# Cross-attention with keys turned before they are stored, a fifth chunk of probabilities turned by DMA, and normalisation once a head

## The reference

```python
q = (x @ Wq + bq); k, v = split(cond @ Wkv + bkv)          # x is layer-normed
q = q / sqrt(64)
q = fq_sym(q, axis=-1); k = fq_sym(k, axis=-1); v = fq_sym(v, axis=2)   # round(x / s) * s, s = max|x| / 127
attn = softmax(q @ k.T); attn = fq_unsigned(attn)          # s = max / 255
x = x + (attn @ v) @ Wp + bp
x = x + causal_self_attention_with_rope(layernorm(x))      # 128 tokens each
x = x + rmsnorm(swiglu_fp4(layernorm(x)))
```

## Time and profile before

| what | value |
|---|---|
| median of 3 executions (range) | 2946.23 us (2945.79 to 2947.63) |
| profiled execution: its time / its span | 2948.09 us / 2946.2 us |
| busy over the span: PE / DVE / ACT / POOL | 2612.4 / 1860.9 / 1033.5 / 553.9 us |
| keys and values end (last DVE instruction ends) | 1412.5 us from the span's start |
| cross-attention, first to last copy of scores | 1458.6 to 2154.8 us |
| last output of the cross-attention | 2175.5 us |

### The profile page before, as it was taken

How to read it: one execution, slowest core, us unless ns; L and a number is a source line. 1 busy time by engine, 2 the same in 40 slices (tenths; PEclk the granted TensorE clock), 3 DMA queues, 4 the chain that set the end, 5 groups by cost and what they waited for, 6 DMA issues and landing times. The chain is left out here.

```text
span 2946.2 us, 42369 instructions
## 1 busy us (share of the span) xinstructions
PE 2612.4 (89%) x16808; PEld 1327.1 (45%) x16808; DVE 1860.9 (63%) x2883; ACT 1033.5 (35%) x920; POOL 553.9 (19%) x208
## 2 busy tenths in 40 slices
PE   6999999999999999999377777777759999499998
PEld 3444444444444444444144444444444476244443
DVE  5855555555555555554489999999944343566663
ACT  3111111111111111111189999999962133211100
POOL 0500000000000000000256546645610721011100
PEclk9999999999999999999689999999989977699999
DMA  6121222212221222212479999999871300300000
GB/s 236 65 79 57 78 85 78 72 67 81 85 78 57 78 85 78 72 67 68 122 172 180 194 208 185 194 199 197 176 224 60 112 1 1 61 15 15 8 0 29
DMA packets 493040, 288.93 MB, mean 98 GB/s; under 512 B 403200, under 2 KB 468992, under 8 KB 488064
## 3 DMA queue, kind: packets, MB, share of 16 engines
q1 hardware_dynamic: 492928, 287.28, 37.5%
HBM read 117.37 MB, written 69.21 MB: 63 GB/s over the span
## 5 line engine op out<-in xcount | busy, mean ns | idle before, releaser
L456 PE MATMUL kv_acc<-kv_whi,kv_xthi 128*128 128x512 f16 x2048 | 776.8, 379 | 5.6 <-DVE kv_xtlo L500 5.6
L456 PE MATMUL kv_acc<-kv_wlo,kv_xthi 128*128 128x512 f16 x2048 | 776.7, 379 | 0.0
L456 PE MATMUL kv_acc<-kv_whi,kv_xtlo 128*128 128x512 f16 x2048 | 776.7, 379 | 0.0
L919 DVE TENSOR_SCALAR_CACHE_REDUCE at_sc<-at_score 128x1024 f32<-128x1024 f32 x512 | 612.0, 1220 | 47.8 <-PE at_score L812 43.4
L1005 ACT ACTIVATE at_sc<-at_sc,at_bias,at_qs 128x4096 uint16<-128x4096 f32 x128 | 484.8, 3791 | 13.4 <-DVE at_bias L931 13.4
L812 PE MATMUL at_score<-at_kt,at_q 128*128 128x512 f16 x1024 | 309.2, 392 | 88.0 <-DVE at_sc L919 43.1
L487 ACT ACTIVATE kv_parts<-kv_key 128x1024 f16<-128x1024 f32 x64 | 67.6, 1057 | 866.6 <-DVE kv_key L525 866.6
L456 PEld LDWEIGHTS kv_acc<-kv_whi,kv_xthi 128*128 128x128 f16 x2048 | 200.5, 98 | 247.9 <-DVE kv_xtlo L500 6.1
L456 PEld LDWEIGHTS kv_acc<-kv_whi,kv_xtlo 128*128 128x128 f16 x2048 | 200.5, 98 | 242.0 <-issue 0.8
L456 PEld LDWEIGHTS kv_acc<-kv_wlo,kv_xthi 128*128 128x128 f16 x2048 | 200.5, 98 | 241.8 <-issue 0.6
L506 DVE SCALAR_TENSOR_TENSOR kv_key<-kv_acc,kv_bias 128x512 f32<-128x512 f32 x128 | 88.5, 692 | 335.1 <-PE kv_acc L456 335.1
(11 more groups left out here) (181 smaller groups left out, 3285.0 us busy)
## 6 DMA issues: line engine op xcount, KB each, us to landing
kv_rows<-in_ctx SPq DMA_DIRECT2D x64, 512.0 KB, 6.0
key_rows<-kv_parts SPq DMA_DIRECT2D x64, 512.0 KB, 2.6
values<-kv_val SPq DMA_DIRECT2D x32, 1024.0 KB, 6.3
x<-values SPq DMA_DIRECT2D x16, 2048.0 KB, 8.8
wq_stage<-in_wkv SPq DMA_DIRECT2D x4, 2048.0 KB, 7.8
x<-in_x SPq DMA_DIRECT2D x2, 2048.0 KB, 8.2
wq_stage<-in_wq SPq DMA_DIRECT2D x2, 2048.0 KB, 13.1
wt_stage<-in_wp SPq DMA_DIRECT2D x2, 2048.0 KB, 10.1
```

Of the source, the lines that this page charges most:

```text
L456: last = nc.tensor.matmul(acc[c][:], a[s][:, k, :], b[:, c, k, :], start=(k == 0 and q == 0), stop=(k == KD - 1 and q == 2))
L919: nc.vector.tensor_scalar(sc[n % 2][:, c * SC:(c + 1) * SC], score[pos % 2][:], 1.0, None, ALU.mult, ALU.max, accum_out=part_max[n % 2][:, ...
```

## The change

- Each key tile is turned by a DMA transpose in SBUF during the projection (`turn_keys`), both tiles of a pair are stored turned (runs of 512 bytes), and the attention loads key quarters with plain DMAs. Head 0's keys are loaded during the projection, those of the last two tiles straight from SBUF (`own_keys`).
- The queries' 64 transposes move into the last pair of the projection, with ACT evicting them.
- The block value_scales is gone. Its reduction stands at the start of the attention; the scales reach all partitions by 16 PE transposes of a broadcast column and two ACT evictions, not through DRAM. DVE, after its first ten copies, and ACT, before its first exponential, wait for the projection's last stores.
- Of each unit a fifth chunk (the last 1024 columns of the second half, the "tail") is turned by a DMA of its own, issued as the last thing of the unit in SP's order. PE turns three chunks instead of four. ACT evicts two or three of them, DVE the middle one in slots with even `n` alone.
- Sum, inverse and output are made once a head (four units), and POOL multiplies by the value scales as it moves the output out.
- The values get a buffer of their own, and head 0's keys take the room of `x`. Before the end `x` is loaded again, as it was before.

```diff
--- before.py
+++ after.py
-            def store_keys(u, s):
+            def turn_keys(u, s):
                 sp.wait_ge(parts_ready, u + 1)
-                dst = kt_d[bass.ds(u, 1)].rearrange("a p n -> (a p) n")
-                sp.dma_start(dst, parts[s][:].rearrange("p h c d -> p (h c d)")).then_inc(k_stored[s], 16)
+                sp.sem_inc(keys_begun, 1)
+                sp.dma_start_transpose(kt[:, :, s * P:(s + 1) * P], parts[s][:].rearrange("p h c d -> p (h c d)"))\
+                    .then_inc(keys_turned[s], 16)
+
+            def store_keys(i):
+                for s in range(2):
+                    sp.wait_ge(keys_turned[s], 16 * (i + 1))
+                    sp.sem_inc(keys_begun, 1)
+                dst = kt_d[:, :, bass.ds(i * (2 * P), 2 * P)].rearrange("h p n -> p h n")
+                sp.dma_start(dst, kt[:]).then_inc(k_stored, 16)
 
             def body(i, first, last):
                 if not last:
                     for s in range(2):
                         sp.wait_ge(lo_ready, 2 * i + s + 1)
                         load(ctx_d[bass.ds(2 * i + 2 + s, 1)].rearrange("a p k n -> (a p) k n"), s)
+                if not first:
+                    sp.wait_ge(k_stored, 16 * i)
+                    sp.sem_inc(keys_begun, 1)
                 for s in range(2):
-                    store_keys(2 * i + s, s)
-                sp.wait_ge(v_ready, 2 * i + 2)
+                    turn_keys(2 * i + s, s)
+                    if last:
+                        heads.own_keys(sp, 2 * i + s, parts[s][:, 0].rearrange("p c d -> p (c d)"))
+                if not last:
+                    store_keys(i)
+                sp.wait_ge(taken, NC * (2 * i + 2))
                 dst = v_d[:, :, bass.ds(2 * i, 2), :].rearrange("h p a d -> p h a d")
                 sp.dma_start(dst, val[:]).then_inc(v_stored, 16)
-
-            each_pair(sp, body)
...
+            quarter = KVT // 8
+            body(0, True, False)
+            for n in range(4):
+                with sp.Fori(n * quarter + 1, min(LAST_PAIR, (n + 1) * quarter + 1)) as i:
+                    body(i, False, False)
+                if n < 3:
+                    sp.wait_ge(k_stored, 16 * (n + 1) * quarter)
+                    heads.keys(sp, 0, 0, (n,))
+            sp.wait_ge(k_stored, 16 * LAST_PAIR)
+            heads.rest(sp, 2 * LAST_PAIR)
+            body(LAST_PAIR, False, True)
...
+            def turn_queries(n):
+                t, g = n // 2, n % 2
+                pe.wait_ge(queries.step, 1 + 4 * T)
+                if n >= 4:
+                    pe.wait_ge(q_t_ready, n - 3)
+                for h in range(8):
+                    last = nc.tensor.transpose(q_bank[n % 4][:, h, :],
+                                               queries.twice[:, t, 8 * g + h, :, :].rearrange("p c d -> p (c d)"),
+                                               ident16[:])
+                last.then_inc(q_turned, 1)
...
+                    if last:
+                        for n in range(T * s, T * s + T):
+                            turn_queries(n)
...
+            def queries_out(n):
+                t, g = n // 2, n % 2
+                act.wait_ge(q_turned, n + 1)
+                nc.scalar.activation(q_t[:, 8 * g:8 * g + 8, t * P:(t + 1) * P], q_bank[n % 4][:], ACT.Copy)\
+                    .then_inc(q_t_ready, 1)
...
-                        act.wait_ge(k_stored[s], 16 * i)
+                        act.wait_ge(keys_turned[s], 16 * i)
...
+    def own_keys(self, sp, u, rows):
+        sp.dma_start_transpose(self.kt[0][:, u * P:(u + 1) * P].unsqueeze(1), rows).then_inc(self.kt_loaded[0], 16)
+
     def keys(self, sp, head, j, quarters):
-        rows, n = self.kt_d.rearrange("u p n -> (u p) n"), NKV // 4
+        n = NKV // 4
         for q in quarters:
-            sp.dma_start_transpose(self.kt[j][:, q * n:(q + 1) * n].unsqueeze(1),
-                                   rows[q * n:(q + 1) * n, bass.ds(head * P, P)]).then_inc(self.kt_loaded[j], 16)
+            sp.dma_start(self.kt[j][:, q * n:(q + 1) * n],
+                         self.kt_d[bass.ds(head, 1), :, q * n:(q + 1) * n].rearrange("a p n -> (a p) n"))\
+                .then_inc(self.kt_loaded[j], 16)
...
-def value_scales(chip, vmax, scale_d, v_scale, twice, q_t, ident32, ident16, stores, heads):
...
-    BANK = (0, 1, 1, 0)
+    BANK = (0, 1, 0)
+    TAIL = 3 * SC
...
+            def turn_tail(g, n):
+                sp.wait_ge(exp_done, EXP0 + 2 * g + 2)
+                sp.sem_inc(dma_begun, 1)
+                sp.wait_ge(tail_summed, DSUM0 + g + 1 - 2)
+                sp.sem_inc(dma_begun, 1)
+                sp.dma_start_transpose(probt_tail[n % 2][:], prob[n % 2][1][:, TAIL:].bitcast(F16)).then_inc(tail_turned[n % 2], 16)
...
+                    turn_tail(i * SLOTS + n, n)
+
+            sp.wait_ge(*stores[1])
+            heads.values(sp, 0)
+            sp.wait_ge(*stores[0])
+            heads.keys(sp, 1, 1, (1, 3, 2, 0))
             each_pair(sp, body)
-            sp.wait_ge(v_quantised, HEADS)
+
+            sp.wait_ge(filled, CH * T * (HEADS - 1))
...
-                elif c == 2:
-                    turns(g, m, 2)
                 elif c == 3:
                     dma_sums(ii, g, m, 0)
                 elif c == 4:
-                    turns(g, m, 3)
+                    turns(g, m, 2)
                 elif c == 5:
                     sums(g, m, 0)
                     sums(g, m, 1)
                 elif c == 6:
                     sums(g, m, 2)
-                    sums(g, m, 3)
...
+                    tail_sums(ii, g, m)
...
+            for k in range(KD):
+                last = nc.tensor.transpose(spread[1][:, k * P:(k + 1) * P], vmax[:, k * P:(k + 1) * P], ident32[:])
+            last.then_inc(vs_turned, 1)
             inputs_ready(0, 0)
             for c in range(CH + AHEAD):
                 scores(c // CH, c // CH, c % CH)
+                if c == 1:
+                    pe.wait_ge(vs_reduced, 1)
+                    for q in range(2):
+                        for k in range(KD):
+                            last = nc.tensor.transpose(spread[q][:, k * P:(k + 1) * P],
+                                                       col[:, q, k:k + 1].to_broadcast((P, P)), ident32[:])
+                        last.then_inc(vs_spread, 1)
+            pe.wait_ge(scales_ready, 2)
...
-                elif c in (4, 5):
-                    dve.wait_ge(turned, TURNED0 + 4 * (h - 2) + 2 * (c - 4) + 2)
+                elif c == 4:
+                    dve.wait_ge(turned, TURNED0 + 3 * (h - 2) + 2)
+                elif c == 5:
+                    dve.wait_ge(turned, TURNED0 + 3 * (h - 2) + 3)
+                    dve.wait_ge(tail_turned[n % 2], DMA0 + 16 * (i * (SLOTS // 2) + n // 2))
...
+            def output(head, j):
+                dve.wait_ge(inv_step, INV0 + 2 * head + 2)
+                dve.wait_ge(dma_summed, DSUM0 + T * (head + 1))
+                dve.wait_ge(o_moved, MOVED0 + head + 1 - 2)
+                nc.vector.tensor_tensor(o_pair[j][:], outp[j], inv[j][:].unsqueeze(2).to_broadcast((P, T, HD)),
+                                        ALU.mult).then_inc(o_taken, 1)
...
+                        if c == 1 and n % 2 == 0 and not (first and n == 0):
+                            turned_out(i * SLOTS + n - 1)
+                        if done is not None and n % T == 0 and c == 5:
+                            total_sum(done, j)
+                        if done is not None and n % T == 0 and c == 6:
+                            inverse(done, j)
+                        if done is not None and n % T == 1 and c == 0:
+                            output(done, j)
...
+            for stored, count in stores:
+                dve.wait_ge(stored, count)
...
+            for q in range(2):
+                act.wait_ge(vs_spread, q + 1)
+                nc.scalar.activation(v_scale[:, q, :], spread[q], ACT.Copy).then_inc(scales_ready, 1)
+            for stored, count in stores:
+                act.wait_ge(stored, count)
...
-                        for k in (0, 2, 3):
+                        for k in ((0, 2) if n % 2 == 0 else (0, 1, 2)):
```

More of the change, by code:

```diff
@@ L391, in gpsimd, with keys_and_values @@
         pool.wait_ge(step, 1 + 4 * T)
-def keys_and_values(chip, ctx_d, rows, rows_loaded, w_hi, w_lo, bias, kt_d, v_d, vmax, ident32, ident16, queries):
+def keys_and_values(chip, ctx_d, rows, rows_loaded, w_hi, w_lo, bias, kt_d, v_d, vmax, ident16, queries, q_t, heads):
     nc = chip.nc
@@ L483, in body @@
                         rows_high(i + s, 1 - s, None if first and s == 0 else NC * u)
+                    if last:
+                        for n in range(T * s, T * s + T):
+                            queries_out(n)
                     act.wait_ge(int_ready, u + 1)
                     if not first:
-                        act.wait_ge(k_stored[s], 16 * i)
+                        act.wait_ge(keys_turned[s], 16 * i)
```

(13 more changed lines are left out.)

242 lines of the change are left out of this document (110 added, 132 removed).

## The result

The changed kernel takes 2953.87 us (median of 18 runs, 2946.39 to 2960.09) and the kernel before, run beside it, 2946.51 (18 runs, 2945.19 to 2949.31). The ratio is 1.0024, with a 95% interval of 1.0017 to 1.0031: slower by 0.24%, where I had forecast 1.4% faster. In the profiled executions the span went from 2946.2 to 2949.9 us.

What follows compares the result with a forecast made beforehand. It took PE to bound the projection and a loop through PE, DVE and ACT the attention's units; 34 + 20 - 15 + 1 = 40 us gained, from 2946.2 to 2906 us, range for 8 in 10 2887 to 2932.

Steps and rivals of the forecast that it cites:

- Start of the attention: Between projection and attention: first score copy 37.5 us earlier, first product with values at about 1452.5, 34 us gained.
- Key turning in the projection: In the projection: 1 MB of transposes a pair added to the DMAs, nothing to PE; taken at 0.
- The loop at 10.46 a unit: In the attention: units of 10.60 and 10.33 us, 0.34 less per unit, over 58 units 20 us gained.
- normalising once a head: In the attention loop on DVE: sum, inverse and output once a head instead of per unit, worth 0.
- The tail's DMA: Once a head the tail queues behind 2 MB of values: 1.1 us lost, for 14 heads 15 us lost.
- The drain: At the kernel's end: one turn and one eviction fewer, 1 us gained.
- Three of the four rivals: Tail not late: 2891, chance 0.25; waits in more slots: 2921 to 2936, 0.13; late in every unit: about 2960, 0.07.
- whether the start gives less: Rival, attention start: scales' detour or stores are waited for, 10 to 15 us less gain, 2916 to 2921; chance 0.10.
- the tail late in every unit: Rival, attention loop: tail's DMA late in all units, slower; about 2960 if it lands 9 us after issue; chance 0.07.

## Why the prediction was wrong

**Start of the attention: right.** First copy at 1422.27 for 1421.0, first product with values at 1453.81 for 1452.5. Of the 34 us, 31.4 stand in the trace at unit 6. The rest is this 1.3 us and 1.4 more on the way to the second head's values, which PE waits for and which come 48.8 us after the first product in place of 47.4. DVE stands 2.46 us at 1480.81 in between, marked "<-issue"; it is at position 7 behind a load of values, and PE waits for the tail at the same moment, so it is a tail's wait, and it lies in the shadow of PE's later wait for POOL:

```profile
1480.39 0.41 PE L884 MATMUL at_outp<-q_twice,at_probt_tail 128*128 128x64 f16 x8 [1.15 <-DMA at_probt_tail<-at_sc]
...
1502.64 1.04 PE L896 MATMUL at_outp<-q_twice,at_probt_dma 128*128 128x64 f16 x16 [4.32 <-POOL q_twice L812]
```

**Key turning in the projection: right.** PE is busy 730.00 of 730.00, DMA share 0.40.

**The loop at 10.46 a unit: right.** The evictions L997 at 1762.69 and 1783.58 are 20.89 us apart, for 20.92 forecast. That normalising once a head is worth nothing was tested and holds. What the sum of this step took for granted was that 57 slots in a row would be such slots.

**The step that failed: an edit to a loop's code was costed by its instructions' time alone.** I had counted what VectorE executes and not where its code lies. Four evictions and some small instructions left the loop, and more left the code ahead of it; the loop became shorter and still lay worse in the blocks. Five stalls: 23 us between units 6 and 63, 26 in the spans, 28 in the medians. Increments alone take them away (48, 96) or bring them back (128), in the kernel before too (76): this cause is shown. The Trainium skill, page "Runtime: NRT & Kernel Launch" (section "Instruction fetch mechanics"), says that a taken branch to code outside the window that is held must fetch it before the engine goes on. The trace agrees: 23 such fetches in place of 1 in the 400 us. I had not weighed it, because the trace of before has 1 fetch in these 400 us; that a shorter body could lose the property didn't occur to me.

**The tail's DMA: the mechanism right, the term mis-sized.** Forecast: the tail lands 9.8 us after the values' issue, 6.5 to 7 after position 3. Measured: 9.66 and 6.9. But I let ScalarE's room take up most of it and came to 1.1 us a head. It is 32.6 over 13 heads, 2.5: 18 us more than the 15 forecast. Even a short wait gives little back: the head around 1746 (units 26 to 30) took 43.13 where 41.78 is its due, 1.35 us lost to a wait of 1.79. And longer waits cost more than they last: the heads around 1840 and 2027 lost 3.5 and 4.3 us to waits of 2.62 and 3.00. Windows of the changed kernel around the waits of 1.79 (first line), 2.62 and 3.00 us:

```profile
1745.00:1755.00 10.00, 6.72 (x86) 4.04 (x84) 8.50 (x17) 8.98 (x6) 9.57 (x2) 1.00 0.85 176
...
1841.00:1849.00 8.00, 6.13 (x59) 3.93 (x60) 6.80 (x15) 5.84 (x6) 7.92 (x2) 0.79 0.73 151
...
2028.00:2036.00 8.00, 6.61 (x56) 4.20 (x57) 6.59 (x13) 5.71 (x4) 7.92 (x2) 0.64 0.74 153
```

The granted clock stays at 1.00 (2.4 GHz) after the first and is 0.79 and 0.64 on the mean after the others, which is partly its lower level, 1.2 GHz. The length of the wait alone doesn't decide it: in the 8 us behind each of the 12 waits the clock is 1.00 after those of 1.19, 1.24 and 1.99 us and after one of 1.79, and 0.79 or less after the other eight, another of 1.79 and one of 1.65 among them. PE's timeline after the wait of 2.62 us shows both:

```profile
1841.29 0.61 PE L849 MATMUL at_score<-at_kt,at_q 128*128 128x512 f16 x2 [1.04 <-DVE at_sc L979]
...
1842.97 1.03 PE L849 MATMUL at_score<-at_kt,at_q 128*128 128x512 f16 x2 [0.61 <-DVE at_sc L979]
1843.80 1.92 PE L867 MATMUL at_turn<-ident,at_sc 128*128 128x128 f16 x16
```

Two score matmuls take 1.03 in place of 0.61, 16 transposes 1.92 in place of 1.07, and the slot after the wait takes 10.98 where 9.70 would be its due. I had priced the wait and not the slower PE behind it. How much of the 18 us is clock and how much the room that ScalarE didn't give wasn't measured apart.

**The drain:** 1 us forecast, none there (791.4 us from the last bias to the end, 791.1 before).

**The sum.** Forecast 40 gained; in its place 31.4 - 34.8 - 0.3 = -3.7. Against the forecast: 23 for the back edges, 18 for the tail and the small waits beside it, 3 at the start, 1 for the drain, less 1 for the loop (57 units at 10.445 for 10.46). Three of the four rivals asked how the tail would behave and one whether the start gives less; none was about code. The rival nearest to the time, the tail late in every unit, had the right side for a wrong reason: in the changed kernel DVE waits for a tail only behind a load of values.

## What to carry to other kernels

Before pricing an edit to a looped kernel, count the loop's instructions as the trace shows them (a copy with an accumulator is two) and look whether instruction DMAs appear at each repetition; if an edit shifts the loop, price a stall of 2 to 7 us per back edge, and try a few idle instructions ahead of it. When a load makes a transfer late, cutting it in two around that transfer beat every reordering, since each reordering only made another due time fail. Price a wait on a chain that is already the bound at most of its length (1.35 us lost to 1.79 here), and more than its length where PE comes out of it at the lower clock (4.3 lost to 3.00), as it did after 8 of 12 waits.

## What the runs showed of the hardware that I had not expected

- A VectorE loop of 287 instructions stalls 4.3 to 6.9 us at each back edge or not at all, by where it begins: with 0 and 128 idle instructions ahead it does, with 48 and 96 it doesn't. A shorter loop can lie worse than a longer one.
- The same misplacement cost 2.7 us per back edge in the kernel before and 5.1 in the changed one. Its first gap is 1.3 to 1.5 us there and 2.6 to 3.8 here. Whether the load on the DMA queues or the place of the missing block makes the difference wasn't tried.
- Straight code of 1290 instructions in the built program, some 1800 with each copy counted as two, was fetched without a long slot at the pairs' starts (30 fetches) at a DMA share of 0.98.
- A semaphore increment on VectorE that nobody waits for takes 90 ns.
